# DLRM tower on one core: GpSimd issues a block of gathers when those of the block ahead have landed

## The reference

```python
e = jnp.stack([tbl_0[ids[:, 0]], ..., tbl_25[ids[:, 25]]], axis=1)        # 512 x 26 x 128
all_emb = jnp.concatenate([bottom_output[:, None, :], e], axis=1)         # 512 x 27 x 128
gram = jnp.einsum('bfd,bgd->bfg', all_emb, all_emb)
z = gram[:, _TRIU_I, _TRIU_J]                                             # 512 x 351
h = jnp.concatenate([z, r_bottom_output], axis=1)                         # 512 x 479
h = jnp.maximum(h @ W_top1 + b_top1, 0.0)                                 # 512
h = jnp.maximum(h @ W_top2 + b_top2, 0.0)                                 # 256
y = h @ W_top3                                                            # 512 x 1
```

## Time and profile before

| | us |
|---|---|
| timed runs, median of 3 | 124.48 (124.38 to 125.06) |
| profiled execution, span from first to last instruction | 165.1 |
| TensorE matmul busy in it | 102.6 (62%) |
| GpSimd busy in it | 81.0 (49%) |
| VectorE busy in it | 58.5 (35%) |
| ScalarE busy in it | 54.4 (33%) |

### The profile page before, as it was taken

How to read it: one execution, slowest core, us unless ns; L and a number is a source line. 1 busy time by engine, 2 the same in 40 slices (tenths; PEclk the granted TensorE clock), 3 DMA queues, 4 the chain that set the end, 5 groups by cost and what they waited for, 6 DMA issues and landing times.

```text
span 165.1 us, 1899 instructions
## 1 busy us (share of the span) xinstructions
PE 102.6 (62%) x700; PEld 90.8 (55%) x700; DVE 58.5 (35%) x109; ACT 54.4 (33%) x78; POOL 81.0 (49%) x81
## 2 busy tenths in 40 slices
PE   6886999959968320000611101006999999999994
PEld 6764788848858310000610000006989999998893
DVE  1279999889712200000100000005554343442210
ACT  3439889696332200000100000005644344351111
POOL 2788888787877777777777777100000000002200
PEclk9999999999999995555555555555999999999999
DMA  3899999999222112112211211102424124104300
GB/s 89 256 237 241 244 240 248 237 265 244 82 63 63 49 48 60 52 48 54 58 48 48 64 48 48 32 0 38 71 50 75 37 31 73 35 4 63 67 4 0
DMA packets 19693, 15.32 MB, mean 93 GB/s; under 512 B 13956, under 2 KB 15872, under 8 KB 19684
## 3 DMA queue, kind: packets, MB, share of 16 engines
q1 hardware_dynamic: 14898, 10.09, 26.9%
q0 software_dynamic: 2416, 4.82, 11.5%
q10 hardware_dynamic: 2370, 0.29, 1.2%
HBM read 13.70 MB, written 1.49 MB: 92 GB/s over the span
## 4 chain that ended last, share of the span: by engine, by line
another core or an unknown queue 36%; PE 19%; POOL 19%; DMA 11%; issue 5%; SPq 4%; DVE 3%; ACTq 1%; ACT 1%
POOL mixed_sb L330 16%; PE banks L434 8%; PE banks L472 5%; DMA products_dram<-products 4%; DMA mixed_sb<-in_mixed_table,mixed_rows_sb 3%; POOL side_sb L322 3%; DMA pairs<-products_dram 3%; PE banks L479 3%; DVE products L572 3%; SPq L307 2%; PE banks L415 2%; DMA side_ids_sb<-in_side_ids 1%; ACTq L295 1%; SPq L295 1%
## 5 line engine op out<-in xcount | busy, mean ns | idle before, releaser
L330 POOL DMA_INDIRECT mixed_sb<-in_mixed_table,mixed_rows_sb x64 | 69.5, 1086 | 19.5 <-issue 19.5
L434 PE MATMUL banks<-turned 128*112 128x104 f32 x256 | 31.4, 278 | 41.1 <-issue 27.0
L434 PEld LDWEIGHTS banks<-turned 128*112 128x112 f32 x256 | 29.5, 193 | 42.5 <-issue 29.7
L572 DVE COPY products<-banks 112x416 f32<-112x416 f32 (+2 forms) x17 | 13.9, 836 | 75.3 <-remote 59.0
L572 ACT COPY products<-banks 112x416 f32<-112x416 f32 (+2 forms) x17 | 14.1, 840 | 77.6 <-remote 59.0
L606 DVE TENSOR_SCALAR one_hot<-lookup_ids_sb,starts_sb 125x512 fp32r<-125x512 int32 x60 | 25.7, 492 | 6.5 <-DMA lookup_ids_sb<-in_lookup_ids 5.0
L398 PE MATMUL banks<-one_hot,high 125*128 125x512 f32 x60 | 24.1, 401 | 2.7 <-DVE low L620 2.7
L400 PE MATMUL banks<-one_hot,low 125*128 125x512 f32 x60 | 23.4, 390 | 0.0
L295 POOL DMA_DIRECT2D products_dram<-products x1 | 0.8, 843 | 45.6 <-ACT products L572 45.6
L415 PE MATMUL banks<-identity,mixed_sb 128*128 128x128 f32 x64 | 11.1, 281 | 14.2 <-issue 10.9
L415 PEld LDWEIGHTS banks<-identity,mixed_sb 128*128 128x128 f32 x64 | 8.0, 146 | 16.1 <-issue 11.7
(11 more groups left out here) (32 smaller groups left out, 74.9 us busy)
## 6 DMA issues: line engine op xcount, KB each, us to landing
raw<-in_tbl SPq DMA_DIRECT2D x6, 448.0 KB
lookup_ids_sb<-in_lookup_ids SPq DMA_DIRECT2D x8, 256.0 KB
raw<-in_tbl SPq DMA_DIRECT2D x2, 560.0 KB
products_dram<-products SPq DMA_DIRECT2D x12, 91.0 KB
mixed_sb<-in_mixed_table,mixed_rows_sb POOLq DMA_INDIRECT x64
pairs<-products_dram SPq DMA_DIRECT2D x16, 39.0 KB
w_sb<-in_w SPq DMA_DIRECT2D x2, 256.0 KB
w_sb<-in_w SPq DMA_DIRECT2D x1, 512.0 KB
```

The source lines that it names most:

```text
L330: pool.indirect_dma_start(mixed_sb[:, n, :], None, mixed_table, bass.IndirectOffsetOnAxis(ap=mixed_rows_sb[:, n:n + 1], axis=0),).then_inc ...
L434: last = pe.matmul(product_ps[0:QUAD * SLOTS, b % 2, k // half, k % half, 0:QUAD * OTHERS], turned[:, t, q, :, :].rearrange("p j f -> p (j ...
L572: copy(products[:, t % 2, :, :, q:q + half].rearrange("p j g q -> p q (j g)"), product_ps[0:QUAD * SLOTS, b % 2, which, 0:half, 0:QUAD * O ...
```

## The change

Ahead of each block of mixed gathers but the first, GpSimd waits until all gathers of the block before it have landed. Destinations, the number of gathers, their order and all other engines' programs are as before. In the changed kernel the mixed gathers stand on line 332.

```diff
                 for b in [b for b in range(BLOCKS) if tile_of(b) == t]:
+                    if b >= 1:
+                        pool.wait_ge(mixed_gathered[b - 1], 16 * GATHERS_OF[b - 1])
                     for n in range(FIRST_GATHER[b], FIRST_GATHER[b + 1]):
                         pool.indirect_dma_start(
                             mixed_sb[:, n, :], None, mixed_table,
```

## The result

The changed kernel takes 154.49 us (median of 4 runs, 153.28 to 158.58), the kernel before 124.77 us (4 runs, 124.38 to 126.03): a ratio of 1.234 with a 95% interval of 1.224 to 1.245, 29.7 us more. The runs of one kernel scatter by 3 to 4% (before took 121.4 to 126.3 us over all sessions), so a ratio here compares only the fast runs of both kernels, and differences of about 1 us are read from the profiles.

What follows compares the result with a forecast made beforehand. The prediction took GpSimd's gather chain and a fixed tail as the bound. Early waits of 13.9 us plus quiet waits of 10.4 us made 24.3 us, added to 124.48 for 148.8 us, range 142 to 155.

Steps and rivals of the forecast that it cites:

- fixed tail: From the last block's turn through products, store and load and last layers to the end: 19.0 us, unchanged.
- the rival that thinner gathers would give it back: Piled-up gathers hold TensorE's instructions, so thinner gathers recover the pause: not slower, about 120 us, chance 3%.
- slack rival: TensorE is the real end and GpSimd has slack: some 10 us of the loss vanish, 138.5 us, chance 8%.
- Quiet waits: Blocks 7 to 16 except 8 and 12: eight waits of 1.3 us each, 10.4 us (8.0 to 12.8).
- Waits under load: Early blocks during table and weight loads: landings of 6.5 us for blocks 1 and 2, 3.0 for block 3.
- The sum 124.2: Kernel before: last gather's end 103.86, landing 1.3 and tail 19.0 us, set against the timed 124.48 us.
- the walk: Block-by-block reckoning of the early gathers: block 6 starts at 63.1 us, 13.9 us later than before.
- The saving beside VectorE: Early gathers: pauses move some away from VectorE's L620, where one takes 2.0 us instead of 0.94; at most 10.5 us.
- the low end of 6.5 us: Early loss up to block 6 if blocks 1, 2, 3, 5 and 6 each wait only the quiet 1.3 us.
- short-landing rival: Landings are short under load too: 13 waits of 1.3 us make 16.9 us, time 141.4 us, chance 6%.
- TensorE: hidden: After block 4 lands, TensorE has 73 us to the last landing for work that took 6.2 + 32.7 us.
- clock rival: New pauses lower TensorE's clock, doubling its 7.0 us on the tail's path: 155.8 us or more, chance 13%.

Runs made afterwards that it cites:

- first profile: Profile of the unchanged kernel before, used for the prediction: span 165.1 us, while its timed runs had a median of 124.48 us.
- early waits alone: Kernel before with GpSimd's waits only ahead of blocks 1 to 5: 141.12 us, ratio 1.125.
- late waits alone: Kernel before with GpSimd's waits only ahead of blocks 6 to 16: 141.53 us, ratio 1.126.
- later weights: Changed kernel with SP issuing the layer weights only after block 4's turn: 155.58 us.
- second profile: Kernel before run and profiled once more with no edit: 124.55 us, span 122.7 us.

## Why the prediction was right, and by how much it fell short

The measured 154.49 us lie 5.7 above the forecast of 148.8, inside the stated range of 142 to 155 but close to its upper end. (The prediction works out its chance of a miss, a little under 2 in 10, with 141 to 157; for the narrower range that it states the chance is larger.) What follows says which terms were too small.

*What bounds the kernel: right.* The gather chain and a fixed tail set the time before and after. The reading that the first profile's pause was not in the timed runs held; the rival that thinner gathers would give it back had nothing to give. The slack rival falls with the table above: the last gather starts 30.0 us later, and the span is 29.8 us longer. The early waits alone and the late waits alone both cost at once.

*Quiet waits: right in number, short in size.* Eight uncovered waits from block 7 on, nothing at blocks 8 and 12. Each was to cost 1.3 us and cost 1.4 to 1.8, 12.2 us in all for 10.4. The bytes are in at 1.0 to 1.2 us after the issue, but whoever waits for the semaphore goes on later: GpSimd after 1.4 us or more, TensorE in the last turn after 133.69 - 132.16 = 1.5 us (the last gather's issue, shown above, ends at 131.21 + 0.95 = 132.16). I had read the end of the bytes and added too little.

*Waits under load: block 1 and 2 right, block 3 short.* 7.2 and 5.8 us for my 6.5 each. For block 3 I expected the loads to be over by 39 us and took 3.0; the landing took 5.5. The windows of the changed kernel show why:

```profile
36.00:38.00 2.00, 0.47 (x3) 0.04 (x1) 1.92 (x4) 1.50 (x2) 1.34 (x2) 1.00 1.07 218
38.00:40.00 2.00, 0.00 (x0) 0.00 (x0) 0.00 (x0) 1.86 (x3) 0.00 (x0) 1.00 1.11 266
40.00:42.00 2.00, 0.00 (x0) 0.00 (x0) 0.00 (x0) 0.00 (x0) 0.00 (x0) 0.77 0.54 131
```

At 38 to 40 us, after the last gather of block 2 was issued, the DMA engines' share is still 1.11. These are the weights, which SP issues behind the last table: with later weights the share in the stretch was 0.13 and just this wait lost 3.7 us.

*The start of the sum: 1.7 us.* In the first profile block 6 started at 49.24 us, in the second one at 47.58. The same loads meet the gathers differently from run to run, and one execution gave me both its pause and a slower early chain. That the sum 124.2 met the median 124.48 was partly luck: against the second profile it had 1.7 us too many in the chain, 0.2 too many in the tail and 0.4 too few in the landing (1.7 us from the last issue to the last turn, for 1.3), and it left out the 1.8 us around the span.

Together: block 6 starts at 65.3 instead of the walk's 63.1, 2.2 us (2.5 for block 3's wait, 0.7 for slower side gathers and 0.7 in small pieces, half of it up to the start of block 1, less 1.7 on block 1, whose issue and landing were shorter than I took); the quiet waits 1.8; the start 1.7; less 0.2 between the last gather and the last turn. That is 5.5 us, and 0.3 more is the median of before, 124.77 in place of 124.48: 5.8 for the 5.7 between 148.8 and 154.5. The saving beside VectorE was in the walk (18.6 us of waits for 13.9 us of delay, so 4.7) and came out at 3.8; the low end of 6.5 us and the 16.9 us of the short-landing rival were reckoned without it. In the runs the waits are 33.6 us and the loss 29.8, for GpSimd's mixed gathers take 4.4 us less than the 69.1 of before and the side gathers 0.6 more:

```profile
L332 POOL DMA_INDIRECT mixed_sb<-in_mixed_table,mixed_rows_sb x64 | 64.7, 1012 | 53.0 <-DMA mixed_sb<-in_mixed_table,mixed_rows_sb 37.5 <-issue 15.6
...
L322 POOL DMA_INDIRECT side_sb<-in_tbl,side_ids_sb x8 | 8.8, 1102 | 4.2 <-issue 2.1 <-DMA side_ids_sb<-in_side_ids 2.1
```

*TensorE: hidden, as said,* with one thing noted. The page's row of the granted clock in 40 slices, and TensorE's above it, are those of a kernel that often stops:

```profile
PE   6939979995069966992846447595978639689994
...
PEclk9986999999857996999687786959999995999999
```

The clock rival came true in the middle and not on the path to the end: TensorE's busy time rose from 100.2 to 113.6 us, but neither the time from the last gather to the last turn nor the tail grew, so the rise lies in time in which it would have waited for gathers. The late waits alone show that the rival is possible all the same: there the fall of the clock met the tail and cost 2.7 us.

## What to carry to other kernels

A wait for one's own DMA ahead of the next issue costs its landing each time, and the landing was as long with one gather in flight as with four: count the waits that nothing else covers and multiply, with one price for the quiet stage and one for the stage under load. With one block more in flight fourteen of fifteen such waits showed no idle time, and what was left of the loss was between nothing and some 2% of the time. Where an engine's issue chain sets the time, look at what lengthens single issues: cutting VectorE's long two-operand operation in four or five made a kernel 1 to 3 us faster than the one before.

## What the runs showed of the hardware that was not expected

- A gather's landing, from the end of its issue to the wait's release, was 1.4 to 1.8 us in the quiet stage of the changed kernel and, over all runs, 4.9 to 8.0 us while loads of tables or weights kept the DMA engines busy (207 to 266 GB/s in the windows shown), for the last of four gathers as for a single one.
- The Trainium skill ("DMA: Bandwidth & Descriptors", "Anatomy of one DMA — SWDGE (gpsimd) path") has about 2.0 us of fixed cost; from the start of the issue it was 0.95 + 1.5 = 2.4 us here when quiet and 5.8 to 9.3 under load, so the traces do not bear out that it is constant.
- A profile can contain a long pause of TensorE that the timed runs do not have: 165.1 us of span in one, 122.7 in the next of the same kernel. The cause stays open.
- A gather beside VectorE's long subtraction took 2.05 us instead of 0.94, with both of its inputs in SBUF; in pieces of a quarter or a fifth no gather took more than 1.30 us on one chip and 1.53 on another. In pieces of an eighth or a tenth one gather took 3.2 us, and that one ran mostly beside one-hots.
